# First graph stage: ReLU and row division moved from ScalarE into VectorE's residual addition

## The chip, the cores and the metric

The kernel runs on one core of a Trainium2 chip. A time is the device time of one execution in microseconds. The engines are PE (TensorE), DVE (VectorE), ACT (ScalarE), POOL (GpSimd) and SP (the queue that issues most transfers); each works through its own instruction list in order, and lists are tied together by semaphores.

## The reference, cut to what matters

`x` is 256 rows of 512 numbers. It passes four residual layers, each on a layer norm of the sum so far. The change lies in the first layer and in what the second takes from it:

```
x = x + graph(layernorm(x))                      # stage 1
x = x + experts(layernorm(x))                    # stage 2
x = x + edge_products(layernorm(x))              # stage 3
x = x + token_experts(layernorm(x))              # stage 4

graph(h):  h = h @ W + b
           adj = 0/1 adjacency of 256 nodes, both directions, + identity
           adj = adj / max(row_sum(adj), 1)
           return relu(w0*h + w1*adj@h + w2*adj@adj@h + w3*adj@adj@adj@h)

layernorm(x) = (x - mean) / sqrt(var + 1e-5)     # along the 512
```

The kernel forms the series without the left factor 1/row_sum: row r of the matrix product holds row_sum(r) times the wanted row, and the division is made after the product. Since row sums are positive, relu(d / r) = relu(d) / r.

## The kernel before, in words

Rows are held as two halves of 128 partitions (h = 0 and 1, `H` = 2), so `xs` and `xn` are 128 x 2 x 512. `xs` is the running sum, `xn` its layer norm. All instruction lists are written out by hand; nothing is scheduled by a planner. What orders the engines is only the place of an instruction in its list and the semaphores it waits for.

Stage 1 ends so. VectorE makes `adj`, its row sums `rsum` (L798), their reciprocals `rinv` (L804) and `cmat`, the divided matrix (L806); TensorE multiplies `adj` by `cmat` (L1182), and again for the third power, and projects x with W in between (L1173). VectorE assembles the series matrix (L824) and adds the bias to the projected halves (L820, L827). The last product, series by projected x, is L1211: four matmuls in TensorE's list (each seen as two in the trace), two for half 0 and two for half 1, into banks 6 and 7; `diff_ps` is raised after each half.

ScalarE then takes the ReLU of each bank with scale `rinv` into `xn` (L538); VectorE adds it to `xs` (L830), takes mean and variance (`variance`, L720 and L721), ScalarE takes the square root (`root_of_variance`, L490). Half 0 is normalised by ScalarE: VectorE makes the reciprocal (L735) and the shift (`centre`, L736), ScalarE one activation (`normalise_first`, L495). Half 1 is normalised by VectorE (`normalise`, L727 and L728). VectorE's order is: add half 0, its statistics, add half 1, `centre`, statistics of half 1, normalise half 1.

TensorE meanwhile runs 22 small matmuls of zeros (`keep_warm`, L1113), then waits for half 0 and transposes it (`transpose_xn`, L1126), 4 more of zeros, and waits for half 1. The routing product (L1220) and the expert products of stage 2 (L1230, then L1254) follow. At the end of stage 2 VectorE adds bank 2 or 3 to `xs` (L963), takes the next layer norm, and splits it with ScalarE into three bf16 parts (L563, L565, L973) that TensorE's gather of rows (L1259) reads.

Of the kernel before, what the change touches and what calls it, by code (L numbers as in the profile page):

```python
# [5 lines left out]
def graph_and_experts(nc, x, src, dst, edge, gnn_w, gnn_b, diff_w, wr, br, wgate, bgate,  # L6
# [4 lines left out]
    P = 128  # L11
    N, D = x.shape
    H = N // P
# [51 lines left out]
    with ExitStack() as ctx:  # L65
# [67 lines left out]
        shift = sb("shift", [P, 1])  # L133
        root = sb("root", [P, H + 1])
        eps = sb("eps", [P, 1])
        small = prod[:].rearrange("p s t u -> p (s t u)")
# [50 lines left out]
        rsum = take([H, 1])  # L187
        rinv = take([H, 1])
        w0sum = take([H, 1])
# [115 lines left out]
        def f2_sb(c):  # L305
# [23 lines left out]
            sem(n) for n in ("cmat_ready", "s2_ps", "s3_ps", "series_ready", "series2_ready"))  # L329
        diff_ps, relu_done = sem("diff_ps"), sem("relu_done")  # L330

# [155 lines left out]
        def _(act):  # L487
            def root_of_variance(n, h):
                act.wait_ge(var_ready, H * n + h + 1)
                nc.scalar.activation(root[:, h:h + 1], mv[:, h, 1:2], ACT.Sqrt, bias=eps[:]).then_inc(root_ready, 1)  # L490

# [42 lines left out]

            act.wait_ge(xnT_a, 2)
            for h in range(H):
                act.wait_ge(diff_ps, h + 1)
                nc.scalar.activation(xn[:, h, :], bank[6 + h], ACT.Relu, scale=rinv[:, h, :]).then_inc(relu_done, 1)  # L538

# [169 lines left out]
        def _(dve):  # L709
# [12 lines left out]

            def normalise(h, of=xs[:]):

                lns[0] += 1
                dve.wait_ge(root_ready, lns[0])
                link(nc.vector.reciprocal(rstd[:, h:h + 1], root[:, h:h + 1]))  # L727
                nc.vector.tensor_scalar(xn[:, h, :], of[:, h, :], mv[:, h, 0:1], rstd[:, h:h + 1],  # L728
                                        ALU.subtract, ALU.mult).then_inc(xn_ready, 1)

            def centre():

                lns[0] += 1
                dve.wait_ge(root_ready, lns[0])
                link(nc.vector.reciprocal(rstd[:, 0:1], root[:, 0:1]))  # L735
                nc.vector.scalar_tensor_tensor(out=shift[:], in0=mv[:, 0, 0:1], scalar=-1.0, in1=rstd[:, 0:1],  # L736
                                               op0=ALU.mult, op1=ALU.mult).then_inc(centred, 1)
# [65 lines left out]
            link(nc.vector.tensor_scalar(rsum, rsum, 1.0, None, ALU.max))  # L803
            link(nc.vector.reciprocal(rinv, rsum))  # L804
            for h in range(H):
# [22 lines left out]
            for h in range(H):  # L828
                dve.wait_ge(relu_done, h + 1)
                link(nc.vector.tensor_tensor(xs[:, h, :], xs[:, h, :], xn[:, h, :], ALU.add))  # L830
                if h:
                    centre()
                variance(h)

            normalise(1)
            copy_xnT(1, xnT)
# [124 lines left out]
            for h in range(H):  # L961
                dve.wait_ge(down_ps, h + 1)
                nc.vector.tensor_tensor(xs[:, h, :], xs[:, h, :], bank[2 + h], ALU.add).then_inc(x2_ready, 1)  # L963
                dve.wait_ge(x2_ready, h + 1)
                variance(h)
                normalise(h)

                for k in range(2):
                    dve.wait_ge(part_a, 2 * h + k + 1)
                    dve.wait_ge(xn_ready, H + h + 2)  # L970
                    if k:
                        dve.wait_ge(part_r, 2 * h + 1)
                    nc.vector.tensor_tensor((rest, xparts[:, 2])[k][:, h, :], (xn, rest)[k][:, h, :], xparts[:, k, h, :], ALU.subtract)\  # L973
                        .then_inc(part_r, 1)
# [493 lines left out]
```

## Time and profile before

| | us |
|---|---|
| median of 3 executions | 277.52 (277.49 to 278.12) |
| span of the profiled execution | 276.2 |
| time around the span (277.52 less 276.2) | 1.3 |
| PE busy | 263.4 (95%) |
| DVE busy | 224.0 (81%) |
| ACT busy | 164.3 (59%) |
| POOL busy | 63.1 (23%) |

The profiled execution has no time of its own beside its span, so the time around the span is taken from the median. Busy time says who works much, not who is waited for. The chain of waits says that: it starts from the last instruction and goes back, step by step, to whatever released it. PE's time there is the time in which the other engines had nothing to do with the end.

### The profile page before, as it was taken

To read this page: it belongs to the slowest core of one execution; us is meant where nothing else is said; L and a number is where in the kernel's file an instruction comes from. 1 tells how busy PE (TensorE), PEld (TensorE's weight loads), DVE (VectorE), ACT (ScalarE), POOL (GpSimd) and SP (SyncE) were. 2 spreads that over 40 slices of the span, in tenths; PEclk is the share of its full clock that TensorE was granted. 3 is DMA by queue.
4 is the path that set the end of the run, shared out by engine and by line. 5 is a ranking of instruction groups with operands and counts; after the bars stand their busy time and mean duration, and the time that the engine had idled before them with its cause. 6 is when DMAs were issued, how large, how long until landed. Compare 5 with 4: busy or idle time off the path is not lost.

```text
span 276.2 us, 5644 instructions
## 1 busy us (share of the span) xinstructions
PE 263.4 (95%) x1631; PEld 185.6 (67%) x1639; DVE 224.0 (81%) x660; ACT 164.3 (59%) x335; POOL 63.1 (23%) x52
## 2 busy tenths in 40 slices
PE   6899999999999899998999999969999999999996
PEld 4566698886444799996678776746656674468633
DVE  5977565199657999999999999999999987655372
ACT  6920551011526699946879786497898839352260
POOL 4000060060006644304769991000000000000000
PEclk9999999999999999999999999977999999999999
DMA  6699990000014557733150002014445428100002
GB/s 203 232 414 405 447 397 12 0 2 1 1 38 129 177 144 252 233 100 101 53 139 17 2 1 76 4 37 141 148 154 152 154 84 320 54 2 2 2 0 76
DMA packets 12592, 33.91 MB, mean 123 GB/s; under 512 B 3345, under 2 KB 3602, under 8 KB 12306
## 3 DMA queue, kind: packets, MB, share of 16 engines
q1 hardware_dynamic: 10482, 26.73, 27.0%
q0 software_dynamic: 2080, 6.82, 8.4%
q8 instruction: 14, 0.23, 0.3%
q14 instruction: 16, 0.13, 0.2%
HBM read 32.50 MB, written 1.05 MB: 121 GB/s over the span
## 4 chain that ended last, share of the span: by engine, by line
PE 85%; DVE 7%; ACT 3%; issue 2%; POOL 1%; ACTq 0%; DVEq 0%; POOLq 0%
PE psum L1276 16%; PE psum L1327 16%; PE psum L1230 10%; PE psum L1330 8%; PE psum L1254 5%; PE psum L1259 4%; PE psum L1282 3%; PE psum L1401 3%; PE psum L1427 3%; PE psum L1173 3%; PE psum L1159 2%; PE psum L1318 2%; PE psum L1182 1%; PE psum L1439 1%; PE psum L1320 1%
## 5 line engine op out<-in xcount | busy, mean ns | idle before, releaser
L460 POOL DMA_INDIRECT big<-xn_rows,big x26 | 51.4, 1975 | 54.4 <-DMA xn_rows<-xn 23.5
L1276 PE MATMUL psum<-big,dst_oh 128*128 128x512 f32 x108 | 51.3, 601 | 0.0
L595 ACT ACTIVATE prod<-edges,coef_b 128x320 f32 (+1 forms) x77 | 42.6, 590 | 11.0 <-PE psum L1330 8.4
L1011 DVE TENSOR_TENSOR prod<-big,prod 128x320 f32<-128x320 f32 (+1 forms) x77 | 40.5, 528 | 0.4 <-DVE big L982 0.2
L1327 PE MATMUL psum<-prod,ident 128*128 128x128 f32 x160 | 31.8, 293 | 0.7 <-DVE prod L1011 0.5
L1327 PEld LDWEIGHTS psum<-prod,ident 128*128 128x128 f32 x160 | 24.5, 190 | 10.0 <-issue 9.2
L1276 PEld LDWEIGHTS psum<-big,dst_oh 128*128 128x128 f32 x108 | 19.1, 195 | 14.9 <-issue 14.9
L1230 PE MATMUL psum<-edges,big 128*128 128x256 f32 x128 | 28.3, 380 | 0.0
L1230 PEld LDWEIGHTS psum<-edges,big 128*128 128x128 f32 x128 | 24.1, 190 | 3.5 <-issue 0.3
L1021 DVE TENSOR_TENSOR big<-big,prod 128x64 f32 (+2 forms) x80 | 26.3, 329 | 0.1
L595 ACT ACTIVATE xparts<-edges,coef_b 128x320 f32 (+1 forms) x45 | 23.9, 582 | 0.9 <-PE psum L1327 0.8
L1011 DVE TENSOR_TENSOR xparts<-big,xparts 128x320 f32<-128x320 f32 (+1 forms) x45 | 23.5, 523 | 0.3 <-ACT src_t L595 0.3
L1330 PE MATMUL psum<-prod,ident 128*128 128x64 f32 (+1 forms) x110 | 19.8, 262 | 0.0
L1327 PE MATMUL psum<-xparts,ident 128*128 128x128 f32 x96 | 19.2, 299 | 0.4 <-DVE xparts L1011 0.4
L595 ACT ACTIVATE xn<-edges,coef_b 128x320 f32 (+1 forms) x32 | 17.7, 589 | 1.7 <-PE psum L1330 1.1
L595 ACT ACTIVATE src_t<-edges,coef_b 128x320 f32 (+1 forms) x30 | 16.3, 579 | 2.4 <-PE psum L1327 2.2
L551 ACT ACTIVATE edges<-psum 128x256 f32<-128x256 f32 x8 | 3.1, 384 | 24.2 <-PE psum L1230 18.6
L1011 DVE TENSOR_TENSOR xn<-big,xn 128x320 f32<-128x320 f32 (+1 forms) x32 | 16.8, 526 | 0.3 <-issue 0.2
L1330 PEld LDWEIGHTS psum<-prod,ident 128*128 128x128 f32 x110 | 16.7, 192 | 0.0
L1327 PEld LDWEIGHTS psum<-xparts,ident 128*128 128x128 f32 x96 | 14.4, 196 | 2.5 <-issue 2.2
L1021 DVE TENSOR_TENSOR big<-big,xparts 128x192 f32 (+2 forms) x48 | 15.9, 331 | 0.2 <-issue 0.2
L1011 DVE TENSOR_TENSOR src_t<-big,src_t 128x320 f32<-128x320 f32 (+1 forms) x30 | 15.6, 520 | 0.4 <-ACT src_t L595 0.4
(215 smaller groups left out, 491.6 us busy)
## 6 DMA issues: line engine op xcount, KB each, us to landing
big<-in_w SPq DMA_DIRECT2D x3, 2048.0 KB, 16.3
edges<-in_f SPq DMA_DIRECT2D x11, 512.0 KB, 3.5
edges<-in_edge SPq DMA_DIRECT2D x1, 3584.0 KB, 23.9
edges<-in_edge SPq DMA_DIRECT2D x1, 2560.0 KB, 23.5
edges<-in_edge SPq DMA_DIRECT2D x5, 512.0 KB
edges<-in_f SPq DMA_DIRECT2D x1, 2560.0 KB, 10.4
big<-in_gnn_w SPq DMA_DIRECT2D x1, 1024.0 KB, 6.2
xs<-in_x SPq DMA_DIRECT2D x1, 512.0 KB, 3.5
```

The lines of the kernel that those rows point to most:

```text
L460: nc.gpsimd.indirect_dma_start(out=x1g[b % 2][:, i, :], out_offset=None, in_=xn_rows, in_offset=bass.IndirectOffsetOnAxis(ap=idx_i[:, 0, F ...
L595: nc.scalar.activation(slot(n)[:, 0:BLOCKS[b], :], segment(edges[:, FIRST[b]:FIRST[b] + BLOCKS[b], :], single_column(words, p)), ACT.Copy, ...
L1011: nc.vector.tensor_tensor(v, segment(xg[:, 0:tiles, :], first_column(words[b], p)), v, ALU.mult).then_inc(mults, 1)
L1021: nc.vector.tensor_tensor(v, v, slot(n)[:, KEPT[b]:BLOCKS[b], :], ALU.add).then_inc(sums, 1)
L1173: last = mm(bank[2 + h], xnT[:, kc, h * P:(h + 1) * P], w_sb[:, kc, :], start=kc == 0, stop=kc == KC - 1)
L1230: last = mm(bank[2 + c % 4][:, n * N:(n + 1) * N], w[:, kc, c * P:(c + 1) * P], xnT[:, kc, :], start=kc == 0, stop=kc == KC - 1)
L1254: last = mm(bank[2 + h], hT[:, c, h * P:(h + 1) * P], w2_sb[:, c, :], start=c == 0, stop=c == HC - 1)
L1259: last = mm(gather_bank(t), src_t[:, h, t * P:(t + 1) * P], xparts[:, k, h, :], start=h == 0 and k == 0, stop=h == H - 1 and k == 2)
L1276: last = mm(bank[2 + h], dst_oh[:, n % DR, h * P:(h + 1) * P], tile_sums(b, t), start=False, stop=False)
L1282: last = mm(bank[2 + h], dst_ohb[:, split_tiles[i], h * P:(h + 1) * P], sum_parts[:, i, k, :], start=False, stop=i == SPLIT - 1 and k == 2)
L1327: last = mm(path_sums(to), ident[:], product[:, 0:PT].rearrange("p t u -> p (t u)"), start=False, stop=True, skip_group_check=True)
L1330: last = mm(more_sums(b, to), ident[:], product[:, PT:KEPT[b]].rearrange("p t u -> p (t u)"), start=False, stop=True, skip_group_check=True)
```

## The change

The division by row sums is put off past the residual addition. ScalarE multiplies `xs` by `rsum` beforehand, half by half, once the row sums are there (L539 of the changed kernel). VectorE then makes one instruction a half, max(bank, 0) + `xs`, straight from PSUM (L837); what stands in `xs` is row_sum times the sum. Its mean and variance are scaled by row_sum and row_sum squared, so ScalarE's square root takes a scale operand `rinv2` = 1/row_sum squared, made by a new VectorE instruction (L810), and VectorE multiplies the reciprocal root by `rinv` (L730), once a half. The addition at the end of stage 2 multiplies `xs` by `rinv` (L971). `rinv` and `rinv2` get rooms of their own, since stage 2's end comes after their old room is used by transfers.

```diff
             def root_of_variance(n, h):
                 act.wait_ge(var_ready, H * n + h + 1)
-                nc.scalar.activation(root[:, h:h + 1], mv[:, h, 1:2], ACT.Sqrt, bias=eps[:]).then_inc(root_ready, 1)
+                scale = rinv2[:, h, :] if n == 1 else 1.0
+                nc.scalar.activation(root[:, h:h + 1], mv[:, h, 1:2], ACT.Sqrt, bias=eps[:], scale=scale).then_inc(root_ready, 1)
...
-            act.wait_ge(xnT_a, 2)
-            for h in range(H):
-                act.wait_ge(diff_ps, h + 1)
-                nc.scalar.activation(xn[:, h, :], bank[6 + h], ACT.Relu, scale=rinv[:, h, :]).then_inc(relu_done, 1)
+            act.wait_ge(inv_ready, 1)
+            for h in range(H):
+                nc.scalar.activation(xs[:, h, :], xs[:, h, :], ACT.Copy, scale=rsum[:, h, :]).then_inc(rows_scaled, 1)
...
-            def normalise(h, of=xs[:]):
+            def inverse(h, by_rows):
 
                 lns[0] += 1
                 dve.wait_ge(root_ready, lns[0])
                 link(nc.vector.reciprocal(rstd[:, h:h + 1], root[:, h:h + 1]))
+                if by_rows:
+                    link(nc.vector.tensor_tensor(rstd[:, h:h + 1], rstd[:, h:h + 1], rinv[:, h, :], ALU.mult))
...
-            link(nc.vector.reciprocal(rinv, rsum))
+            link(nc.vector.reciprocal(rinv[:], rsum))
+            nc.vector.tensor_tensor(rinv2[:], rinv[:], rinv[:], ALU.mult).then_inc(inv_ready, 1)
...
             for h in range(H):
-                dve.wait_ge(relu_done, h + 1)
-                link(nc.vector.tensor_tensor(xs[:, h, :], xs[:, h, :], xn[:, h, :], ALU.add))
+                dve.wait_ge(rows_scaled, h + 1)
+                dve.wait_ge(diff_ps, h + 1)
+                link(nc.vector.scalar_tensor_tensor(out=xs[:, h, :], in0=bank[6 + h], scalar=0.0, in1=xs[:, h, :],
+                                                    op0=ALU.max, op1=ALU.add))
                 if h:
-                    centre()
+                    centre(True)
                 variance(h)
 
-            normalise(1)
+            normalise(1, by_rows=True)
...
-                nc.vector.tensor_tensor(xs[:, h, :], xs[:, h, :], bank[2 + h], ALU.add).then_inc(x2_ready, 1)
+                nc.vector.scalar_tensor_tensor(out=xs[:, h, :], in0=xs[:, h, :], scalar=rinv[:, h, :], in1=bank[2 + h],
+                                               op0=ALU.mult, op1=ALU.add).then_inc(x2_ready, 1)
```

VectorE's list where the row sums become reciprocals, before (`edges` names the room that holds `adj`, `rsum`, `rinv` and `cmat`):

```order
L803 TENSOR_SCALAR edges<-edges 128x2 [waits adj_ready]
L804 RECIPROCAL edges<-edges 128x2 [waits chain]
L806 TENSOR_SCALAR edges<-edges 128x256 [waits chain]
L806 TENSOR_SCALAR edges<-edges 128x256
L807 TENSOR_SCALAR xparts<-edges 128x512
```

The same place in the changed kernel:

```order
L808 TENSOR_SCALAR edges<-edges 128x2 [waits adj_ready]
L809 RECIPROCAL rinv<-edges 128x2 [waits chain]
L810 TENSOR_TENSOR rinv<-rinv 128x2 [waits chain]
L812 TENSOR_SCALAR edges<-edges,rinv 128x256 x2
L813 TENSOR_SCALAR xparts<-edges 128x512
```

One instruction is new, between the reciprocal and the two that TensorE's product waits for; none of these waits for it.

VectorE's list at the end of stage 1, before:

```order
L827 TENSOR_TENSOR edges<-psum,edges 128x512 [waits h_ps]
L830 TENSOR_TENSOR xs<-xs,xn 128x512 [waits relu_done]
L720 BN_STATS stats<-xs 128x6 [waits chain]
L721 BN_AGGR mv<-stats 128x2 [waits chain]
L830 TENSOR_TENSOR xs<-xs,xn 128x512 [waits relu_done]
L735 RECIPROCAL rstd<-root 128x1 [waits root_ready,chain]
L736 SCALAR_TENSOR_TENSOR shift<-mv,rstd 128x1 [waits chain]
```

And in the changed kernel:

```order
L833 TENSOR_TENSOR edges<-psum,edges 128x512 [waits h_ps]
L837 SCALAR_TENSOR_TENSOR xs<-psum,xs 128x512 [waits diff_ps,rows_scaled]
L721 BN_STATS stats<-xs 128x6 [waits chain]
L722 BN_AGGR mv<-stats 128x2 [waits chain]
L837 SCALAR_TENSOR_TENSOR xs<-psum,xs 128x512 [waits diff_ps,rows_scaled]
L728 RECIPROCAL rstd<-root 128x1 [waits root_ready,chain]
L730 TENSOR_TENSOR rstd<-rstd,rinv 128x1 [waits chain]
L741 SCALAR_TENSOR_TENSOR shift<-mv,rstd 128x1 [waits chain]
```

The order is the same; the two additions wait for TensorE and no longer for ScalarE's ReLU, and the multiplication by `rinv` stands between the reciprocal and the shift. The same instruction is added between reciprocal and normalisation of half 1.

## Rows read from the trace of the kernel before

**Rows 1.** The page's chain that ended last, share of the span by engine.

```profile
PE 85%; DVE 7%; ACT 3%; issue 2%; POOL 1%; ACTq 0%; DVEq 0%; POOLq 0%
```

**Rows 2.** Chain of waits in order of time, 26 to 37 us: start, us, what.

```profile
29.22 0.70 DVE xs L830
...
30.87 0.70 DVE xs L830
...
34.60 1.70 PE psum L1220 x16
```

**Rows 3.** Timeline of the end of stage 1: start, us, engine, line, [idle before <-releaser].

```profile
28.50 0.69 ACT L538 ACTIVATE xn<-psum,edges 128x512 f32<-128x512 f32 x1 [11.78 <-PE psum L1211]
...
29.95 0.70 DVE L720 BATCH_NORM_STATS2 stats<-xs 128x6 f32<-128x512 f32 x1
29.95 2.56 PE L1113 MATMUL psum<-iota_w,zero_b 128*128 128x256 bf16 x22
...
30.15 0.69 ACT L538 ACTIVATE xn<-psum,edges 128x512 f32<-128x512 f32 x1 [0.96 <-PE psum L1211]
30.68 0.18 DVE L721 BATCH_NORM_AGGREGATE mv<-stats 128x2 f32<-128x6 f32 x1
...
31.60 0.17 DVE L735 RECIPROCAL rstd<-root 128x1 f32<-128x1 f32 x1
31.80 0.16 DVE L736 SCALAR_TENSOR_TENSOR shift<-mv,rstd 128x1 f32<-128x1 f32 x1
31.88 0.69 DVE L720 BATCH_NORM_STATS2 stats<-xs 128x6 f32<-128x512 f32 x1
32.00 0.81 ACT L495 ACTIVATE xn<-xs,shift,rstd 128x512 f32<-128x512 f32 x1 [0.81 <-DVE shift L736]
...
32.81 0.29 ACT L490 ACTIVATE root<-mv,eps 128x1 f32<-128x1 f32 x1
...
33.34 0.55 DVE L728 TENSOR_SCALAR xn<-xs,mv,rstd 128x512 f32<-128x512 f32 x1
...
33.94 0.42 PEld L1126 LDWEIGHTS psum<-ident,xn 128*128 128x128 f32 x4 [0.27 <-DVE xn L728]
```

**Rows 4.** Timeline where the row sums become reciprocals.

```profile
19.52 0.17 DVE L804 RECIPROCAL edges<-edges 128x2 f32<-128x2 f32 x1
19.72 0.62 DVE L806 TENSOR_SCALAR edges<-edges 128x256 f32<-128x256 f32 x2
20.13 1.59 PEld L1182 LDWEIGHTS psum<-edges 128*128 128x128 f32 x8 [0.72 <-DVE edges L806]
```

**Rows 5.** Single lines: duration ns min/median/max, first and last start us, forms.

```profile
L963 DVE TENSOR_TENSOR xs<-xs,psum x2: 689/689/689, 72.4 to 79.3; 128x512 f32<-128x512 f32 x2
L1073 DVE SCALAR_TENSOR_TENSOR big<-psum,row_room x2: 692/692/692, 255.4 to 259.8; 128x512 f32<-128x512 f32 x2
L817 DVE SCALAR_TENSOR_TENSOR xparts<-psum,edges,xparts x2: 476/480/484, 22.5 to 22.9; 128x256 f32<-128x256 f32 x2
L824 DVE TENSOR_TENSOR xparts<-xparts,psum x2: 414/418/422, 25.6 to 25.9; 128x256 f32<-128x256 f32 x2
L490 ACT ACTIVATE root<-mv,eps x8: 278/294/295, 6.9 to 243.2; 128x1 f32<-128x1 f32 x8
L559 ACT ACTIVATE root<-eps x1: 203/203/203, 72.1 to 72.1; 128x1 f32<-128x1 f32 x1
```

**Rows 6.** Timeline at the end of stage 2.

```profile
77.24 0.69 DVE L973 TENSOR_TENSOR xparts<-prod,xparts 128x512 bf16<-128x512 f32 x1 [0.69 <-ACT xparts L565]
...
79.30 10.31 PE L1259 MATMUL psum<-xparts,src_t 128*128 128x512 bf16 x47
...
84.11 0.69 DVE L973 TENSOR_TENSOR xparts<-prod,xparts 128x512 bf16<-128x512 f32 x1 [0.69 <-ACT xparts L565]
```

**Rows 7.** Windows of PE: stretch, us and PE busy (x), granted clock, DMA share, GB/s.

```profile
184.00:186.00 2.00, 0.98 (x4) 0.50 0.11 16
186.00:188.00 2.00, 2.00 (x9) 0.50 0.68 246
190.00:192.00 2.00, 2.00 (x9) 0.88 0.52 207
```

More of the change, by code:

```diff
@@ L134, in graph_and_experts @@
         root = sb("root", [P, H + 1])
+        rinv = sb("rinv", [P, H, 1])
+        rinv2 = sb("rinv2", [P, H, 1])
         eps = sb("eps", [P, 1])
@@ L187, in graph_and_experts @@
         rsum = take([H, 1])
-        rinv = take([H, 1])
         w0sum = take([H, 1])
@@ L329, in graph_and_experts @@
             sem(n) for n in ("cmat_ready", "s2_ps", "s3_ps", "series_ready", "series2_ready"))
-        diff_ps, relu_done = sem("diff_ps"), sem("relu_done")
+        diff_ps, inv_ready, rows_scaled = sem("diff_ps"), sem("inv_ready"), sem("rows_scaled")
         logit_ps, route_in, exp_done, tw_ready, twT_ps, twT_ready = (
@@ L727, in normalise, with centre @@
                 link(nc.vector.reciprocal(rstd[:, h:h + 1], root[:, h:h + 1]))
+                if by_rows:
+                    link(nc.vector.tensor_tensor(rstd[:, h:h + 1], rstd[:, h:h + 1], rinv[:, h, :], ALU.mult))
+            def normalise(h, of=xs[:], by_rows=False):
+                inverse(h, by_rows)
                 nc.vector.tensor_scalar(xn[:, h, :], of[:, h, :], mv[:, h, 0:1], rstd[:, h:h + 1],
                                         ALU.subtract, ALU.mult).then_inc(xn_ready, 1)
[L731 to L735, printed above, removed]
+            def centre(by_rows=False):
+                inverse(0, by_rows)
                 nc.vector.scalar_tensor_tensor(out=shift[:], in0=mv[:, 0, 0:1], scalar=-1.0, in1=rstd[:, 0:1],
```

## The prediction, made before the changed kernel ran

> **What bounds the kernel now.** I read the chain of waits first, because the question of this change is whether the place that it touches is waited for. Over the whole span the chain is PE's to 85% [rows 1]: most of the time nothing but TensorE's work sets the end. The chain in order of time between 26 and 37 us shows the exception. TensorE's last product of stage 1 releases ScalarE's first ReLU, at 28.50 us [rows 3]; from there to the routing product, 34.60 us, the chain runs through ScalarE and VectorE, with both residual additions in it, at 29.22 and at 30.87 [rows 2]. So both additions are on the path, though only half 0's ReLU is: the second ReLU (30.15) is over before VectorE comes to half 1's addition [rows 2, 3].
>
> The timeline of the same stretch is read next, because two half-row chains and TensorE's filler run side by side there. The reader should see three things in it [rows 3]. Half 0's normalised rows come at 32.81 (32.00 + 0.81). TensorE's 22 matmuls of zeros begin at 29.95 and last 2.56 us, to 32.51 as their ends are modelled, so they hide nearly all of that wait; only about 0.3 us of it shows. And half 1's rows are what TensorE waits for last: they start at 33.34, and its transposes begin at 33.94, after an idle 0.27. Everything behind (transposes, routing, expert products) is one TensorE piece after another. What the change is worth is therefore how much earlier half 1's transposes start, not how much earlier half 0's do.
>
> **The change part by part.**
>
> *ReLU out of the chain.* Before, the first addition starts at 29.22, 0.72 us after ScalarE's ReLU at 28.50. Now VectorE starts when TensorE's half is done; I take ScalarE's start for it too, 28.50. The new instruction reads PSUM and one SBUF tensor, and its constant is immediate. The same kind at the same size takes 692 ns (L1073), a plain addition from PSUM 689 (L963) [rows 5], and the addition from SBUF 0.70 in the chain [rows 2]. So its duration is that of the old one, and each later step keeps its old distance. Distances from start to start, read off the old rows [rows 2, 3]: addition to statistics 0.73, statistics to aggregate 0.73, aggregate to next addition 0.19, addition to reciprocal 0.73, small linked instruction to the next 0.20.
>
> The Trainium skill, page "Perfetto Trace Analysis", section "Optimizing Scalar/DVE Operations", speaks against moving the PSUM read: it gives VectorE about 60 ns of access overhead on SBUF and about 125 on PSUM. Here L963 with a PSUM operand is no longer than L830 without one, so the trace does not agree at this form; by the page, an estimate, the two additions would lose some 0.13 us together and the sum below would be near zero. I go by the rows.
>
> *The new order of the chain.* Addition 0 at 28.50, statistics 29.23, aggregate 29.96, free for addition 1 at 30.15. Addition 1 now also waits for half 1's product; ScalarE's second ReLU, which waited for just that, began at 30.15 [rows 3]. The two meet: VectorE no longer waits for ScalarE, but TensorE is late next, to the hundredth. Addition 1 runs at 30.15 in place of 30.87: 0.72 us won, and this one number is the whole gain. Moving addition 0 still earlier would win nothing.
>
> *Multiplication by `rinv`, twice.* It is linked on both sides, so it costs one small linked step, 0.20 (31.60 to 31.80 [rows 3]), in half 0 between reciprocal and shift, and in half 1 between reciprocal and normalisation. Both lie in series for half 1, because half 1's statistics stand behind the shift: 0.40. Half 0: reciprocal 30.88, multiplication 31.08, shift 31.28, ScalarE's normalisation 31.48 to 32.29, in place of 32.81: 0.52 earlier. Half 1: statistics at 31.36 (0.08 behind the shift [rows 3]), over before 32.29.
>
> *Scale operand of the square root.* Adding a bias operand to this instruction is worth 294 against 203 ns (L490 against L559) [rows 5]; I take the same 0.09 for a second operand, bounded by nothing and by twice that. Half 0's root is covered: it would end near 30.5, before addition 1 does. Half 1's is not: ScalarE starts it at 32.29, when its own normalisation ends, and it ends at 32.67 in place of 33.10. Reciprocal 32.71, multiplication 32.91, normalisation 33.11 in place of 33.34 [rows 3]. Half 1 is thus 0.72 − 0.40 − 0.09 = 0.23 us earlier.
>
> *TensorE's filler.* The 22 matmuls end at 32.51 or, since the next one can begin while the last is under way, up to 0.2 earlier. Half 0's rows at 32.29 then no longer keep TensorE waiting: the filler takes the wait's place and half 0's transposes move by 0.3 to 0.5 only. They and the 4 matmuls of zeros behind them end by 33.5, before half 1's rows come (33.71), so this costs nothing now. It would be the bound if half 1 were won by more than 0.4.
>
> *`rinv2`.* One instruction of 128x2 in front of `cmat`. TensorE's product loads its first `cmat`-side weights at 20.13, idle 0.72 until VectorE's L806 [rows 4], so VectorE is waited for there, and a delay passes on: TensorE's next pieces are tied end to end up to L1211. Nothing waits for `rinv2` itself, so its price is the distance to an unlinked next instruction, 0.08 (31.80 to 31.88 [rows 3]). From above it is bounded by a linked step, 0.20; from below by nothing, if TensorE's preceding matmul covers it. I take 0.08, the row of the same situation.
>
> The skill's page "VectorE: DVE Perf Modes", section "The DRAIN you can't avoid", says that the next instruction does not start until the pipeline has emptied. By that the price is a whole small instruction, as an estimate of the same size as the linked step, and the sum is 0.12 less. L736 lasts 0.16 and its successor starts 0.08 after it, so the trace does not agree for this pair.
>
> *ScalarE's two multiplications of `xs`.* About 0.7 each like the ReLUs. ScalarE is idle for 11.78 us before 28.50 [rows 3]; the row sums are there by 19.7, so these end near 21.3. Nothing. Without that cover the first addition would wait, up to 1.4 us.
>
> *The addition at the end of stage 2.* A pointer scalar in a three-operand instruction: 480 against 418 ns at 128x256 (L817, L824) [rows 5], so 0.06 a half. Half 0's parts are ready at 77.93 (77.24 + 0.69), a microsecond before TensorE's gather at 79.30. Half 1's last part is ready at 84.80, and is read by the last 16 of 48 gather matmuls of 0.22 us each (10.31 / 47), from about 86.3 [rows 6]. Both covered: nothing.
>
> **Sum.** 0.23 − 0.08 = 0.15 us earlier at 34.6 us, and TensorE's chain carries it to the end. Span 276.2 − 0.15 = 276.05; with 1.3 around it that is the median of 277.52 less 0.15, so 277.4 us. With the unknown terms at their good ends (root operand 0, `rinv2` 0, VectorE starting 0.05 sooner) it is 0.37, at their bad ends (0.18, 0.20) 0.72 − 0.40 − 0.18 − 0.20 = −0.06. So between 0.4 us faster and 0.1 slower.
>
> **Rivals.**
> 1. *The wait is only replaced.* VectorE's chain gets three small linked steps for one ReLU, `rinv2` costs its full 0.20, and the new instruction is dearer than its rows by the 0.06 of a three-operand form in each of two places. Then 0.72 − 0.40 − 0.09 − 0.20 − 0.12 = −0.09: 277.6. For it: every added piece is linked. Against it: L1073 has no such surplus.
> 2. *The gain is larger*, because half 0 releases TensorE too: if addition 1 starts with its product well before 30.15 and the root's operand is free, half 1 moves up to the 0.4 where the filler binds, 277.1. Against it: the second ReLU's start shows when the product is there.
> 3. *The low-clock stretch shifts.* From 184 to about 191 us TensorE is granted 0.50 (1.2 GHz), after it had been busy for only half of 184 to 186, and is back near 2.4 GHz in 190 to 192 [rows 7]. If a start earlier by some tenths makes the low stretch last longer, each further microsecond of TensorE work in it costs 0.5. It decides from 1.7 us more on: 0.85 us and 0.3% slower, 278.4. The same in reverse gives up to 3 us faster, by half of the six busy microseconds. For it: the stretch exists and the three times before differ by 0.6. Against it: all engines' work before it moves by one and the same shift, so nothing in the pattern changes.
>
> **How the numbers follow.** What a measurement of this kernel can tell from no change is about 0.3%, 0.83 us. Forecast 56%, rival 1 20%, rival 2 10%, rival 3 slower 7% and faster 7%. Only rival 3 passes the bound: faster 7%, same 86%, slower 7%. The range: the forecast and rivals 1 and 2 span 277.1 to 277.6; the three times before scatter to 0.6 above their lowest, so a median may lie 0.4 to either side: 276.7 to 278.1.
>
> **What would show it.** In the changed profile: L837 first at about 28.5 and again at 30.1 to 30.2, each near 0.69; L730 twice, each 0.20 ahead of its successor; the second root (L492) near 0.38; half 0's transposes right behind the filler, with no idle time; half 1's transposes at about 33.8 where they were at 33.94; the first `cmat` instruction 0.08 later than 19.72; the gather with no idle time in it. It would be wrong if addition 1 starts much before or after 30.15, if L837 is over 0.75, or if the difference of the spans arises behind 37 us.

## The result, and the profile after

| | before | after |
|---|---|---|
| median, us | 277.51 | 283.30 |
| profiled execution, us | | 283.28 |
| its span | 276.2 | 281.5 |
| PE busy | 263.4 | 266.7 |
| DVE busy | 224.0 | 224.4 |
| POOL busy | 63.1 | 82.0 |

The changed kernel is slower: 283.30 against 277.51 us, ratio 1.020 (1.019 to 1.021). One execution of 383.38 us is left out, as disturbed. The forecast was 277.4, with 276.7 to 278.1 around it: wrong. The two spans differ by 5.3 us; most other executions of the kernel before have a span of 275.7, so the profiled one of it was half a microsecond long, and the loss is 5.8. The time around the span is 1.8 us (283.28 less 281.5), not the 1.3 taken ahead of the prediction, which set the median beside the span of a longer execution; the forecast of the median was made from a difference and does not hang on it.

The chain by engine, on the page after, shows it before any detail:

```profile
PE 62%; POOL 15%; DVE 11%; issue 3%; ACT 3%; DVEq 2%; DMA 2%; POOLq 0%; ACTq 0%; SPq 0%
```

PE had 85% and POOL 1% [rows 1]. GpSimd, an engine that the change does not touch, now sets 15% of the span. The chain in order of time, after, around the place (start, us, what):

```profile
142.12 40.96 POOL big L461
183.09 1.25 POOLq L65
184.34 0.30 issue
184.64 3.75 DMA big<-xn_rows,big
188.59 0.50 DVE xparts L1020
```

One gather of rows (`gather_rows`, L460 before, L461 after: GpSimd takes 128 row numbers of `idx_i` and issues the transfer of these rows) lasts 40.96 us. Two more stand behind it, and the last one's rows land at 188.4. Stage 3 goes through its edges in three blocks; VectorE is in the second from 126 to 182, while GpSimd gathers the rows of the third. VectorE's list there, after (the last bracket is the idle time before, and who ended it):

```profile
181.81 0.45 DVE L1030 TENSOR_TENSOR big<-big,prod 128x256 f32 x1
188.59 0.49 DVE L1020 TENSOR_TENSOR xparts<-big,xparts 128x320 f32<-128x320 f32 x1 [6.32 <-DMA big<-xn_rows,big]
```

and before:

```profile
181.97 0.42 DVE L1021 TENSOR_TENSOR big<-big,prod 128x256 f32 x1
182.31 0.48 DVE L1011 TENSOR_TENSOR xparts<-big,xparts 128x320 f32<-128x320 f32 x1
```

VectorE waits 6.32 us for rows that were long there before, and the whole loss arises here. Up to the wait VectorE is 0.16 us earlier than before (181.81 against 181.97). That this is nearly the forecast 0.15 is chance: at 163 it is 0.03 earlier (162.99 against 163.02), and the other 0.13 is a short pause of VectorE that is missing now, as the rows below show. GpSimd's timeline from 132 to 200 us, before:

```profile
134.13 4.91 POOL L460 DMA_INDIRECT big<-xn_rows,big  x1 [1.79 <-DVE prod L1011]
139.34 1.07 POOL L460 DMA_INDIRECT big<-xn_rows,big  x1 [0.30 <-DVE prod L1011]
140.71 1.10 POOL L460 DMA_INDIRECT big<-xn_rows,big  x1 [0.30 <-issue]
142.13 1.42 POOL L460 DMA_INDIRECT big<-xn_rows,big  x1 [0.32 <-DVE xparts L1011]
144.74 20.59 POOL L460 DMA_INDIRECT big<-xn_rows,big  x1 [1.19 <-DVE prod L1011]
165.63 1.03 POOL L460 DMA_INDIRECT big<-xn_rows,big  x1 [0.30 <-DVE prod L1011]
```

and after:

```profile
134.12 4.04 POOL L461 DMA_INDIRECT big<-xn_rows,big  x1 [1.79 <-DVE prod L1020]
138.46 1.06 POOL L461 DMA_INDIRECT big<-xn_rows,big  x1 [0.30 <-DVE prod L1020]
139.83 1.10 POOL L461 DMA_INDIRECT big<-xn_rows,big  x1 [0.30 <-issue]
142.12 40.96 POOL L461 DMA_INDIRECT big<-xn_rows,big  x1 [1.19 <-DVE xparts L1020]
183.39 0.95 POOL L461 DMA_INDIRECT big<-xn_rows,big  x1 [0.30 <-issue]
184.64 0.94 POOL L461 DMA_INDIRECT big<-xn_rows,big  x1 [0.30 <-issue]
```

Most gathers last 0.94 to 1.11 us. Even before, two of them were held for 4.91 and 20.59 us, unseen, because their rows were needed only at 182. VectorE works in this stretch on nothing but pairs of a multiplication (L1011 before, L1020 after) and an addition (L1021, L1030), both with two inputs from SBUF, one pair each 0.87 us with no gap. A multiplication is followed by the next addition 0.53 us later, except at a few places, called pauses here. Before, these are the two in the stretch:

```profile
137.60 0.61 DVE L1011 TENSOR_TENSOR prod<-big,prod 128x448 f32<-128x448 f32 x1
...
163.89 0.62 DVE L1011 TENSOR_TENSOR src_t<-big,src_t 128x448 f32<-128x448 f32 x1
164.55 0.43 DVE L1021 TENSOR_TENSOR big<-big,src_t 128x256 f32 x1
```

with the first one's addition 0.69 behind it, at 138.29, and the second's 0.66. The held gathers end at 139.04 and 165.33, about 0.75 us behind each late addition (0.75 and 0.78). After:

```profile
136.72 0.62 DVE L1020 TENSOR_TENSOR prod<-big,prod 128x448 f32<-128x448 f32 x1
137.41 0.43 DVE L1030 TENSOR_TENSOR big<-big,xn 128x256 f32 x1
...
162.99 0.64 DVE L1020 TENSOR_TENSOR src_t<-big,src_t 128x448 f32<-128x448 f32 x1
163.52 0.44 DVE L1030 TENSOR_TENSOR big<-big,xparts 128x256 f32 x1
```

The first pause is there, one pair earlier (0.69), and the first gather ends at 138.16, again 0.75 behind it. The second is gone (0.53), and the gather is held until VectorE runs dry at 182.

Which gather is held is a question of its own, for not every gather beside such pairs is. The gathers at 142.13 before and at 142.12 after begin at the same place of a pair, 0.02 us behind a multiplication, with no pause near; one lasts 1.42 and the other 40.96. What differs in the rows is how long GpSimd had been idle: 0.32 and 1.19 us. In this stretch, over the fourteen traces of this case, no gather that began up to 0.85 us behind the end of the one before it was held, and each one held began 1.19 us or more behind; five others that began 1.18 us or more behind it, beside the same pairs, were over in 1.09 to 1.75. So idle time of GpSimd goes with being held, but is not enough for it, and no run changed it alone. In the first block, from 99 to 114 us, seven gathers beside pairs of 128x320 and 128x64, as dense, last 1.09 to 1.11.

Stage 1 itself, after, at the places of [rows 3] and [rows 4]:

```profile
19.81 0.16 DVE L810 TENSOR_TENSOR rinv<-rinv 128x2 f32<-128x2 f32 x1
19.89 0.61 DVE L812 TENSOR_SCALAR edges<-edges,rinv 128x256 f32<-128x256 f32 x2
...
28.67 0.69 DVE L837 SCALAR_TENSOR_TENSOR xs<-psum,xs 128x512 f32<-128x512 f32 x1 [1.36 <-PE psum L1220]
...
30.34 0.39 ACT L492 ACTIVATE root<-mv,eps,rinv 128x1 f32<-128x1 f32 x1 [9.00 <-DVE mv L722]
30.39 0.69 DVE L837 SCALAR_TENSOR_TENSOR xs<-psum,xs 128x512 f32<-128x512 f32 x1
...
31.31 0.16 DVE L730 TENSOR_TENSOR rstd<-rstd,rinv 128x1 f32<-128x1 f32 x1
31.50 0.16 DVE L741 SCALAR_TENSOR_TENSOR shift<-mv,rstd 128x1 f32<-128x1 f32 x1
...
32.56 0.42 PEld L1135 LDWEIGHTS psum<-ident,xn 128*128 128x128 f32 x4 [0.17 <-ACT xn L497]
...
33.93 0.42 PEld L1135 LDWEIGHTS psum<-ident,xn 128*128 128x128 f32 x4 [0.55 <-DVE xn L735]
```

This execution is 0.09 us behind already before anything of the change runs, at the row sums. Half 1's transposes start at 33.93 against 33.94: 0.10 us won, where 0.15 were forecast.

### The profile page after: what moved, and what is told of

It is laid out like the page before. It is cut to its first block, busy times and chain, and to the rows that moved or that the text cites. A ratio compares the mean times of both kernels' runs of the same rounds, so it can differ in the third digit from the quotient of the medians.

```text
span 281.5 us, 5648 instructions
## 1 busy us (share of the span) xinstructions
PE 266.7 (95%) x1631; PEld 186.9 (66%) x1639; DVE 224.4 (80%) x663; ACT 164.6 (58%) x335; POOL 82.0 (29%) x52
## 4 chain that ended last, share of the span: by engine, by line
PE 62%; POOL 15%; DVE 11%; issue 3%; ACT 3%; DVEq 2%; DMA 2%; POOLq 0%; ACTq 0%; SPq 0%
POOL big L461 15%; PE psum L1239 10%; PE psum L1336 9%; PE psum L1285 9%; PE psum L1263 5%; DVE big L1030 4%; PE psum L1268 4%; PE psum L1339 4%; PE psum L1291 3%; PE psum L1410 3%; PE psum L1436 3%; PE psum L1182 2%; PE psum L1168 2%; DVEq L1020 1%; DMA big<-xn_rows,big 1%
## 5 line engine op out<-in xcount | busy, mean ns | idle before, releaser
L461 POOL DMA_INDIRECT big<-xn_rows,big x26 | 70.2, 2701 | 54.5 <-DMA xn_rows<-xn 23.5
L1285 PE MATMUL psum<-big,dst_oh 128*128 128x512 f32 x108 | 52.3, 611 | 0.2 <-DVE big L1030 0.2
L1020 DVE TENSOR_TENSOR prod<-big,prod 128x320 f32<-128x320 f32 (+1 forms) x77 | 41.4, 538 | 0.4 <-DVE big L991 0.2
L1020 DVE TENSOR_TENSOR xparts<-big,xparts 128x320 f32<-128x320 f32 (+1 forms) x45 | 24.0, 533 | 6.3 <-DMA big<-xn_rows,big 6.3
L1030 DVE TENSOR_TENSOR big<-big,prod 128x64 f32 (+2 forms) x80 | 27.2, 340 | 0.4 <-issue 0.2
L1239 PEld LDWEIGHTS psum<-edges,big 128*128 128x128 f32 x128 | 24.1, 190 | 3.5 <-issue 0.3
L596 ACT ACTIVATE xparts<-edges,coef_b 128x320 f32 (+1 forms) x45 | 24.1, 581 | 1.7 <-PE psum L1336 0.7
L1336 PE MATMUL psum<-xparts,ident 128*128 128x128 f32 x96 | 20.0, 303 | 2.3 <-DVE xparts L1020 2.3
L1020 DVE TENSOR_TENSOR xn<-big,xn 128x320 f32<-128x320 f32 (+1 forms) x32 | 17.2, 537 | 0.0
L1030 DVE TENSOR_TENSOR big<-big,xparts 128x192 f32 (+2 forms) x48 | 16.3, 340 | 0.0
L1020 DVE TENSOR_TENSOR src_t<-big,src_t 128x320 f32<-128x320 f32 (+1 forms) x30 | 15.9, 530 | 0.0
```

Source lines behind the costliest of these rows:

```text
L461: nc.gpsimd.indirect_dma_start(out=x1g[b % 2][:, i, :], out_offset=None, in_=xn_rows, in_offset=bass.IndirectOffsetOnAxis(ap=idx_i[:, 0, F ...
L596: nc.scalar.activation(slot(n)[:, 0:BLOCKS[b], :], segment(edges[:, FIRST[b]:FIRST[b] + BLOCKS[b], :], single_column(words, p)), ACT.Copy, ...
L1020: nc.vector.tensor_tensor(v, segment(xg[:, 0:tiles, :], first_column(words[b], p)), v, ALU.mult).then_inc(mults, 1)
L1030: nc.vector.tensor_tensor(v, v, slot(n)[:, KEPT[b]:BLOCKS[b], :], ALU.add).then_inc(sums, 1)
L1239: last = mm(bank[2 + c % 4][:, n * N:(n + 1) * N], w[:, kc, c * P:(c + 1) * P], xnT[:, kc, :], start=kc == 0, stop=kc == KC - 1)
L1285: last = mm(bank[2 + h], dst_oh[:, n % DR, h * P:(h + 1) * P], tile_sums(b, t), start=False, stop=False)
```

## The experiments

VectorE executes the changed list with five more instructions ahead of this stretch, two waits (one a half, for a second semaphore) and three small computations (L810, and L730 twice). Counted in the trace, register and wait instructions with them, the two pauses of the kernel before come right behind VectorE's 575th and 703rd instruction, 128 apart. In the changed kernel the pause at 137.41 is behind the 575th again. A pair takes five instructions early in the stretch and four later, register instructions included: the shift by five is one whole pair at the first place and not at the second, where the 703rd is now a multiplication, with the instruction that readies the next addition behind it, and no pause shows. An 8 KB transfer starts on the DMA queue for instructions 0.7 to 0.9 us behind each late addition (at 138.99 and 165.45 before, 138.09 after), and one 0.8 behind the start of the changed kernel's 703rd (163.77). The trace does not tell for which engine it is, and two more such transfers in the same stretch have no pause beside them. So the theory: *VectorE's two-input instructions lock GpSimd out; a held gather ends only at a pause, and the pauses stand where VectorE's instruction list is loaded on; five more instructions take the second one away.* Its rivals: the pattern depends on the moment at which the engines come there, on the moment at which a gather starts, on the new rooms of `rinv`, or on what the new instructions do.

**Pauses put in on purpose, both kernels.** One small linked memset behind four of the pairs:

```diff
+        spare = sb("spare", [P, P])
...
                 add(n)
+                if n - NP in (12, 20, 28, 36):
+                    link(nc.vector.memset(spare[:], 0.0))
```

> The changed kernel, with four linked 128x128 memsets of a spare tile put into VectorE's list of the second edge block (behind the additions of paths 12, 20, 28 and 36), each a moment in which VectorE runs no instruction with two SBUF inputs. Theory A (a row gather of GpSimd starves for 41 us, 142.12 to 183.08, because VectorE's back-to-back two-input instructions leave it no turn): the gather that starts near 142 ends within a microsecond or so of the pause behind path 20, no GpSimd gather is longer than 8 us, the 6.3 us wait of VectorE for gathered rows at 182 is gone, and the time is 277.3 to 278.5 (four pauses at about 0.2 us each, partly covered). Theory B (the loss comes from something else in the change, and the long gather is only a symptom): the time stays near 283 or goes to 284.

> The kernel before with the same four pauses. Theory A: its 20.6 us gather (144.74) shortens to a few us, but nothing waited for it, so only the pauses are paid: 277.5 to 278.4. Against the changed kernel with pauses this gives what the change itself is worth: 0 to 0.2 us. Theory B: 277.5 to 278.4 as well; the pair then differs by 5 us.

Measured: 279.28 us for the changed kernel, 1.0065 (1.0048 to 1.0081) of before, and 279.09 for the kernel before, 1.0058 (1.0041 to 1.0074). GpSimd's timeline of the changed kernel with pauses:

```profile
142.70 4.37 POOL L462 DMA_INDIRECT big<-xn_rows,big  x1 [1.72 <-DVE xparts L1021]
147.37 1.04 POOL L462 DMA_INDIRECT big<-xn_rows,big  x1 [0.30 <-DVE xn L1021]
```

The gather that lasted 40.96 ends at 147.07, and VectorE's wait is gone. The two kernels, 5.8 apart, are now 0.19 apart, the changed one still the slower. The pauses cost more than expected, 1.6 us in the kernel before: each keeps the next multiplication back, 0.80 behind the addition (146.63 against 145.83) in place of 0.34. That the gather is what costs the time is shown; why it is held is not yet.

**The same kernels a little later.** One more matmul of zeros in TensorE's list, behind half 1's transposes:

```diff
             transpose_xn(1)
+            keep_warm(bank[5], 1)
```

> The kernel before with one more matmul of zeros between half 1's transposes and the routing product: everything behind 34 us starts 0.1 us later, nothing else differs. Theory A': which gather starves, and how long, hangs on the moment at which the engines meet, so a shift of 0.1 us may change it: any of 277.6, 280 or 283 is possible, and the lengths of the two long gathers (4.9 and 20.6 us) change. Theory C (the pattern is fixed by the semaphores, so only the change's own edits can alter it): 277.6 and the same two lengths within 0.2 us.

> The changed kernel with the same one matmul more. Theory A': the 41 us gather may break up, to 277.6 to 283.4, with other lengths. Theory C: 283.4 and a gather of 41 us.

Measured: 277.59 us, 1.001 (1.0001 to 1.002), and 283.21, 1.0208 (1.0191 to 1.0225). In the first profile, of an execution of 279.93 us, all came 2.5 us late, and yet the gathers' lengths are those of before to the hundredth:

```profile
136.64 4.91 POOL L460 DMA_INDIRECT big<-xn_rows,big  x1 [1.79 <-DVE prod L1011]
...
147.25 20.59 POOL L460 DMA_INDIRECT big<-xn_rows,big  x1 [1.19 <-DVE prod L1011]
```

In the second they are 4.03 and 40.95. The moment in the execution does not matter. Both engines moved together here, so how they stand to each other is the next question.

**Another start for the gathers.** They wait for the pair's addition in place of its multiplication:

```diff
                     if b == 2 and i >= 2:
-                        pool.wait_ge(mults, NP + 3 * (i - 1))
+                        pool.wait_ge(sums, NP + 3 * (i - 1))
```

> The changed kernel, where the gathers of the third edge block wait for VectorE's addition of a path in place of its multiplication, an instruction later. In both traces the gathers that starve start 13 to 26 ns behind the start of a VectorE multiplication, and those that start in its middle take about 1.1 us. Theory G (the moment of the start decides whether a gather starves, the pause only when it ends): starts move to some 0.35 us behind a multiplication's start, no gather is over 2 us, and the time is 277.2 to 277.6. If the start does not matter: gathers of 4 and 41 us again, 283.3.

Measured: 281.86 us, 1.016 (1.0143 to 1.0177). The rival fell: a gather that starts 0.35 us behind a multiplication's start is held as one that starts beside it.

```profile
143.36 1.09 POOL L461 DMA_INDIRECT big<-xn_rows,big  x1 [1.18 <-DVE big L1030]
145.98 37.13 POOL L461 DMA_INDIRECT big<-xn_rows,big  x1 [1.52 <-DVE big L1030]
183.41 0.95 POOL L461 DMA_INDIRECT big<-xn_rows,big  x1 [0.30 <-issue]
```

The gather at 143.36 began at the same place of a pair, 0.34 behind a multiplication, and was not held: the place does not decide it either way. One gather fewer is left behind the held one (0.95 and the 0.30 before it), and the kernel is 1.4 us faster than the changed one: what counts is how many gathers are left when VectorE runs dry.

**The kernel before with five more instructions, the changed one with five fewer.** VectorE sets 16 cells of a small table with 16 memsets at 38 us, 95 us ahead of the stretch. It gets five idle ones more (on unused cells), or makes the same table with 11:

```diff
-            for i in range(G):
-                for j in range(G):
-                    last = nc.vector.memset(low[:, i, j:j + 1], 1.0 if j < i else 0.0)
+            pieces = [(i, lo, hi) for i in range(G) for lo, hi in ((0, i), (i, G)) if lo < hi]
...
+            for k in range(21 - len(pieces)):
+                nc.vector.memset(small[:, 2000 + k:2001 + k], 0.0)
+            for i, lo, hi in pieces:
+                last = nc.vector.memset(low[:, i, lo:hi], 1.0 if lo < i else 0.0)
```

> The kernel before, with five more tiny memsets of unused cells in VectorE's routing piece (21 in place of 16). The changed kernel has five more VectorE instructions ahead of the edge blocks than the one before (three computations, two waits); nothing else of it is here. Theory D (the only pauses in VectorE's back-to-back stream in the second edge block are of 0.15 us each about 128 instructions apart, at the same time as 8 KB fetches of its program; they give GpSimd its turn, and where the program is shifted by five instructions the second pause vanishes): the pattern of the changed kernel appears, gathers of 4.0 and 41 us, and 283.2 to 283.5. Rival E (scaled rows, operand rooms or the end of stage 2 do it): 277.5 to 277.7, gathers of 4.9 and 20.6 us.

> The changed kernel with the same routing constants written by 11 memsets in place of 16, so that VectorE's program is as long ahead of the edge blocks as that of the kernel before. Theory D: gathers of 4.9 and 20.6 us, and 277.3 to 277.6. Rival E: 283.1 to 283.4, gathers of 4.0 and 41 us.

Measured: the kernel before with five more takes 283.26 us, 1.0207 (1.019 to 1.0224), with nothing of the change in it. Its timeline is that of the changed kernel:

```profile
134.22 4.03 POOL L460 DMA_INDIRECT big<-xn_rows,big  x1 [1.79 <-DVE prod L1017]
...
142.22 40.95 POOL L460 DMA_INDIRECT big<-xn_rows,big  x1 [1.19 <-DVE xparts L1017]
```

The changed kernel with five fewer takes 277.38 us, 0.9994 (0.9985 to 1.0004), with the lengths of before and the late addition back (164.53, 0.66 behind its multiplication):

```profile
134.11 4.90 POOL L461 DMA_INDIRECT big<-xn_rows,big  x1 [1.79 <-DVE prod L1026]
...
144.72 20.58 POOL L461 DMA_INDIRECT big<-xn_rows,big  x1 [1.19 <-DVE prod L1026]
```

So the number of instructions ahead of the stretch is the cause, in both directions. 277.48 less 277.38, 0.10 us, is about what the change is worth by itself; the transposes at 33.93 say the same. The times alone would not carry it: the interval reaches 1.0004, five small memsets are saved as well, and in the pair with pauses the changed kernel was 0.19 the slower.

**The rooms alone.** `rinv` and `rinv2` get rooms of their own in the kernel before, and nothing else changes:

```diff
+        rinv = sb("rinv", [P, H, 1])
+        rinv2 = sb("rinv2", [P, H, 1])
...
-            link(nc.vector.reciprocal(rinv, rsum))
+            link(nc.vector.reciprocal(rinv[:], rsum))
```

> The kernel before with the changed kernel's two new rooms for the inverse row sums (the addresses behind them move by the same bytes), and nothing else. Theory D: 277.5, gathers of 4.9 and 20.6 us. Rival F (addresses decide the port's turns): 283.

Measured: 277.50 us, 1.0001 (0.999 to 1.0011), gathers of 4.91 and 20.58. The two rooms, and the addresses that they shift, play no part.

**Other counts.** The same loop with 31 memsets in the changed kernel (15 more than it has, so 20 instructions more than before), and with 17 and 20 in the kernel before (one and four more):

> The changed kernel with 15 more tiny memsets of unused cells in the routing piece, 20 VectorE instructions more than before ahead of the edge blocks. In the traces the pauses stand where the 575th and the 703rd executed VectorE instruction come, 128 apart in both kernels; with 5 instructions to a pair (multiplication and addition) early in the block and 4 later, the pause shows where it falls between an addition's register operation and the addition. 20 is a whole number of pairs in both parts, so theory D: both pauses are back, four or five pairs earlier (near 133 and 159.5), no gather is over some 25 us, and the time is 277.3 to 277.8, although work was added. Rival (the length only matters as it is in one of the two kernels): 283.3.

> The kernel before with one tiny memset more. Theory D: an offset of 1 is not a whole number of pairs in either part, so neither pause shows; the gather that starts near 134.2 starves until VectorE runs dry near 182, five more gathers of 1.25 us each stand behind it, and the time is 285 to 290. Rival: a single instruction of some 15 ns changes nothing, 277.5.

> The kernel before with four more memsets: a whole pair in the later part (pause near 163 stays), not in the early one (pause near 137.6 gone). Theory D: the gather that starts near 134.2 lasts until about 163.7, the ones behind it follow in 1 to 1.5 us each unless one starves anew (then 284 and more); without that 277.5 to 278.5. Rival: as the kernel before, 4.9 and 20.6 us.

Measured: 277.24 us, 0.9993 (0.9975 to 1.0011); 287.08, 1.0335 (1.0314 to 1.0356), from two executions; 277.51, 1.0002 (0.999 to 1.0014). One idle memset in the kernel before costs 9.6 us: neither pause is left, the first gather is held from the start, and five are left behind it.

```profile
134.22 48.79 POOL L460 DMA_INDIRECT big<-xn_rows,big  x1 [1.79 <-DVE prod L1017]
183.31 0.95 POOL L460 DMA_INDIRECT big<-xn_rows,big  x1 [0.30 <-issue]
```

With 20 the second pause is there as expected and frees the gathers at 164.48. That the first gather would be held until then missed: it ended after 4.37 us, at 138.50, behind a weaker pause at the 575th instruction (the multiplication at 137.68, 0.41 behind the addition in place of 0.34). Over all fourteen traces, each pause in this stretch that no memset or gather made lies right behind the 575th or the 703rd instruction, and every held gather ended 0.74 to 0.85 us behind a pause, a memset or the end of VectorE's last instruction. With 31 the pauses lie at 134.11 and 159.52 (additions 0.68 and 0.67 behind), and the held gather of 24.07 us ends at 160.97. This has the lowest median of all kernels here, but within its interval it is equal to before.

**One instruction of another kind.** One memset, not linked, behind one pair of the changed kernel:

```diff
                 add(n)
+                if n - NP in (28,):
+                    nc.vector.memset(spare[:], 0.0)
```

> The changed kernel with a single 128x128 memset of a spare tile behind the addition of path 28 of the second edge block (near 151), with no wait on it, so that VectorE is never idle. Theory H (it is the two-SBUF-input form of VectorE's instructions that keeps GpSimd out, so any other instruction lets it in): the 41 us gather ends near 151 (9 us), the two behind it take 1 to 1.5 us, and the time is 277.4 to 277.9. If only idle time lets GpSimd in: 41 us again and 283.4.

Measured: 277.40 us, 1.000 (0.9982 to 1.0018). VectorE and GpSimd there:

```profile
152.23 0.42 DVE L1031 TENSOR_TENSOR big<-big,xparts 128x256 f32 x1
152.62 0.17 DVE L1039 MEMSET spare<- 128x128 f32 x1
152.71 0.56 DVE L1021 TENSOR_TENSOR src_t<-big,src_t 128x448 f32<-128x448 f32 x1
```

```profile
142.13 11.34 POOL L462 DMA_INDIRECT big<-xn_rows,big  x1 [1.19 <-DVE xparts L1021]
```

The gather ends at 153.47, 0.76 us behind the next multiplication, and the loss of 5.8 us is gone for one memset that delays the next multiplication by 0.14 (152.71 − 152.23 = 0.48 in place of 0.34). VectorE is never idle there, so a held gather does not need VectorE to stand still. Whether it is the other kind of instruction that lets it in, or only the 0.14 us without the start of a two-input one, about as long as a pause, is not separated.

## Why the prediction was wrong

*Stage 1, nearly right.* Addition 0 was forecast at 28.50, with 0.08 for `rinv2` and 0.09 for the offset of this execution 28.67, and came at 28.67. It lasts 0.69 as the rows said. The surplus of some 65 ns that the Trainium skill, page "Perfetto Trace Analysis", section "Optimizing Scalar/DVE Operations", puts on a PSUM operand did not show. The linked multiplication costs 0.19 and 0.20 (31.31 to 31.50, 33.13 to 33.33), the root 0.39 against 0.29: operand 0.10, forecast 0.09. The term of `rinv2` is 0.08 as taken: `cmat` starts 0.08 behind L810. The prediction set the Trainium skill, page "VectorE: DVE Perf Modes", section "The DRAIN you can't avoid", against this term; the same paragraph of it goes on that an instruction which is not held starts earlier, so the page does not contradict the 0.08. The term that was off is addition 1: forecast 30.32 in the same way, measured 30.39, 0.27 behind the aggregate in place of 0.19. The chain shows a wait instruction at 30.31 ahead of it (it now waits for two semaphores); no run took this apart. Half 0's transposes came right behind the filler (32.57, its end modelled at 32.68), with their weight loads held 0.17 by half 0's rows at 32.52, and half 1's rows were what TensorE waited for. ScalarE's multiplications of `xs` ran in its idle time at 20.0. The additions at the end of stage 2 last 748 ns against 689, the 0.06 forecast, and VectorE's last part at 84.16 kept no matmul waiting. Sum: 0.10 against 0.15.

*The step that failed.* That the time went the other way has nothing to do with these hundredths. It is the Sum's "TensorE's chain carries it to the end", and the reason given against rival 3, "all engines' work before it moves by one and the same shift, so nothing in the pattern changes". All work did move by one shift. What changed was the number of instructions before it, which the prediction counted only as durations. TensorE's chain did not carry the gain to the end: VectorE, which feeds it, waited 6.32 us for the rows behind a gather held for 40.96, and in place of a gain of 0.15 us there was a loss of 5.8. The chain of before gave POOL 1%, and so its gathers were never read: they had lasted 4.91 and 20.59 us in the timeline, against 0.95, and the long one ended some 17 us ahead of the need (165.3 against 182.3). A slack that ends at a rare event of another engine should have been priced: with the event gone, the gathers end when VectorE runs dry, which is what happened.

*The rivals.* Rivals 1 and 2 concerned tenths, and stage 1's rows, 0.10 us earlier, lie between them; the interval around 277.38 is too wide to tell. Rival 3's mechanism did not make the loss: two executions of the changed kernel with a mean granted clock of 0.981 and 0.994 both took 283.16. The low stretch (1.2 GHz) did shift and grow, but it begins behind the start of the wait at 182:

```profile
184.00:186.00 2.00, 1.29 (x7) 0.87 0.67 193
186.00:188.00 2.00, 1.33 (x6) 0.50 0.57 176
188.00:190.00 2.00, 0.74 (x2) 0.50 0.00 0
```

These windows of PE (as in [rows 7]: busy, granted clock) show TensorE idle for most of 188 to 190, for want of VectorE's rows, and at 0.50 from 186 on. The low stretch lasts until about 195 here. In the changed kernel with one matmul more it is over by 188 (0.63 in 184 to 186, 0.51 in 186 to 188, 1.00 behind), and the spans are 281.5 and 281.4: the clock adds nothing to the loss that can be seen. The prediction's own last sentence named the sign, "if the difference of the spans arises behind 37 us"; it put no chance on it, and 0.86 on no change was far too sure.

*What the theory rests on.* Shown: the held gather costs the time (pauses on purpose); neither the moment, its start within a pair nor the rooms decide it; the number of VectorE's instructions before the stretch does, both ways; one other instruction in the stretch frees it. The Trainium skill, page "SBUF — State Buffer", section "Who interferes with whom", has the rule that would have raised the question: VectorE and GpSimd share a pair of SBUF ports, held for a whole instruction, and a VectorE instruction with two SBUF inputs contends with a GpSimd instruction that reads SBUF. The trace agrees with the contention, not with the extent: by the rule the loser waits until the other's instruction ends, here 0.6 us, and the rows show it waiting over some 47 pairs (40.96 / 0.87), though the lock should be free between any two of them. Only argued: that the two engines contend for a port at all (what is measured is lengths), and that the pauses are the loading of VectorE's instructions (their distance of 128 instructions speaks for it, the 8 KB transfers near them weakly). Left open: why some gathers beside the same pairs are not held (1.42 at 142.13 before), nor those of the first block; why the direct multiplications (L1006, from 126 to 132 us, two SBUF inputs as well, the addition 0.60 behind each) leave the gathers beside them at 0.95; and what exactly ends a held gather about 0.75 us behind a pause.

## What to carry to other kernels

Read the lengths of every engine's instructions of one kind, not only those of the engines on the chain: here a kind that lasts 0.95 us in one place lasted 20 in another, and its slack hung on an event of another engine that ended the holding. Where VectorE runs two-input SBUF instructions back to back for tens of microseconds beside GpSimd's indirect transfers, look for held transfers, and try one cheap instruction of another kind between them: one unlinked memset gave back 5.8 us here, while four linked ones cost the kernel before 1.6. Issuing the transfers before the stretch begins is another way, which no run here tried. And when a small edit moves a kernel by per cents, add or take away the same number of idle instructions in the kernel before: it tells in one run whether the edit's content or only its length did it.

## What the runs showed of the hardware

- A gather issued by GpSimd, 0.95 us long by itself, lasted 4.0, 4.9, 11.3, 20.6, 24.1, 37.1, 41.0 and 48.8 us beside VectorE's back-to-back two-input instructions, depending on where VectorE's pauses fell. Others beside the same instructions, above all those begun 0.30 us behind the gather before, lasted 0.94 to 1.42.
- Two pauses of about 0.15 us in VectorE's stream, 128 executed instructions apart, decided 5.8 us (the second one gone) and 9.6 us (both gone).
- Five idle memsets made the kernel before 2.07% slower, one made it 3.35% slower (two executions), four changed nothing; nor did twenty instructions more (the changed kernel with fifteen more memsets).
- A pointer as the scale of ScalarE's 128x1 root cost 0.10 us (0.29 to 0.39), and VectorE's 128x512 addition with a pointer scalar takes 0.06 more than the plain one (689 to 748 ns), while the form with an immediate and a PSUM operand takes no more (0.69).
